# Sorted experts in two halves of the tokens, and the expert's register loaded a block ahead

## What is computed

```python
def _L1_ffn_ref(x, W_router, b_router, W1, b1, W2, b2):      # 8 experts, top 2, D_FF = 512
    logits = x @ W_router + b_router
    # top 2 experts of each token, softmax over their two logits -> weights
    ...
    # for each expert: y = relu(x @ W1[e] + b1[e]) @ W2[e] + b2[e]
    # output = sum over the two chosen experts of weight * y
...
x = _layernorm(x + _L1_attn_ref(x, ...), axis=-1)
x = _layernorm(x + _L1_ffn_ref(x, L1_ffn_W_router, L1_ffn_b_router, L1_ffn_W1, L1_ffn_b1, L1_ffn_W2, L1_ffn_b2), axis=-1)
```

## Time and profile before

| | us |
|---|---|
| median of 3 runs | 1996.16 (1993.97 to 1998.4) |
| the profiled execution, its own time | 1996.44 |
| its span in the trace | 1994.7 |
| of that, ahead of the last layer | 1784.6 |
| the last layer | 210.1 |

### The profile page before, as it was taken

The page is one execution under the profiler, slowest core; times in us unless marked ns, Lnnn a source line. Parts: engine busy times, 40 slices in busy tenths (PEclk is TensorE's granted clock), DMA queues, the critical chain, the costliest instruction groups (busy, mean ns, idle before and its releaser), DMA issues. The chain is left out here.

```text
span 1994.7 us, 42267 instructions
## 1 busy us (share of the span) xinstructions
PE 1715.1 (86%) x15741; PEld 1456.9 (73%) x15741; DVE 1396.7 (70%) x3204; ACT 991.3 (50%) x2605; POOL 600.6 (30%) x978
## 2 busy tenths in 40 slices
PE   3599999899999999999994597999999999997593
PEld 2487778778787787887773465788888888886583
DVE  4688777787777877778774676566666666654466
ACT  2255555455555555555552223565666666541242
POOL 6255335553355543455532000000000000013441
PEclk9799999999999999999997698999999999997697
DMA  5122232223331334313230101990000000011122
GB/s 191 52 70 62 73 83 65 52 62 72 83 73 44 69 75 73 83 43 73 64 73 22 75 1 30 148 5 1 1 1 2 1 1 2 1 61 57 50 59 82
DMA packets 148047, 106.71 MB, mean 53 GB/s; under 512 B 32972, under 2 KB 136216, under 8 KB 146952
## 3 DMA queue, kind: packets, MB, share of 16 engines
q1 hardware_dynamic: 145576, 99.37, 24.0%
q0 software_dynamic: 2272, 4.67, 0.7%
HBM read 86.91 MB, written 17.10 MB: 52 GB/s over the span
## 5 line engine op out<-in xcount | busy, mean ns | idle before, releaser
L577 POOL TENSOR_TENSOR kfull<-kt,pair_rows 128x512 f32<-128x512 f32 x128 | 144.0, 1125 | 515.2 <-ACT kt L365 505.3
L345 PE MATMUL ps<-xT,taps 128*128 128x128 f32 x2176 | 294.1, 278 | 0.1
L345 PEld LDWEIGHTS ps<-xT,taps 128*128 128x128 f32 x2176 | 274.7, 196 | 7.8 <-issue 7.4
L830 ACT COPY wt<-ps 32x128 f32<-32x128 f32 x512 | 131.7, 257 | 260.0 <-PE ps L726 253.5
L1560 DVE TENSOR_REDUCE b_nmax<-ps 128x1 f32<-128x128 f32 (+7 forms) x256 | 180.5, 752 | 73.0 <-PE ps L1397 73.0
L873 DVE TENSOR_TENSOR prod<-ps,mt 128x128 f32<-128x128 f32 x512 | 147.3, 288 | 75.2 <-PE ps L737 60.1
L726 PE MATMUL ps<-ident,w 128*128 128x128 f32 x512 | 162.3, 317 | 34.2 <-ACT wt L830 17.7
L1537 POOL COPY b_spread<-b_inv 128x256 f32<-128x256 f32 x64 | 25.8, 403 | 512.9 <-DVE b_inv L1563 512.9
L876 DVE TENSOR_REDUCE w<-prod 128x32 f32<-128x128 f32 x512 | 146.6, 286 | 17.5
L726 PEld LDWEIGHTS ps<-ident,w 128*128 128x128 f32 x512 | 87.9, 172 | 84.9 <-DVE w L876 73.7
L1489 ACT ACTIVATE b_prob_long<-ps,b_nmax 128x1024 f32<-128x1024 f32 (+3 forms) x128 | 121.4, 953 | 55.7 <-DVE b_nmax L1560 55.7
(11 more groups left out here) (280 smaller groups left out, 3839.0 us busy)
## 6 DMA issues: line engine op xcount, KB each, us to landing
decay<-ends_dram SPq DMA_DIRECT2D x256, 128.0 KB, 5.6
gn<-near_dram SPq DMA_DIRECT2D x34, 384.0 KB, 7.0
rr<-rates_dram SPq DMA_DIRECT2D x34, 256.0 KB, 4.5
sq<-rstd_dram SPq DMA_DIRECT2D x17, 512.0 KB, 3.7
slots_dram<-zero SPq DMA_DIRECT2D x1, 8704.0 KB, 62.5
wtap<-in_taps SPq DMA_DIRECT2D x4, 1024.0 KB, 11.7
f_w<-in_f_w SPq DMA_DIRECT2D x2, 2048.0 KB, 11.5
s_xb<-slots_dram SPq DMA_DIRECT2D x39, 64.5 KB
```

What stands on the lines that cost most here:

```text
L345: mm = pe.matmul(part, lhsT=taps[:, tap, t * P:(t + 1) * P], rhs=xT[:, :, columns(at_next) - LOOK + tap:columns(at_next) - LOOK + tap + TS ...
L577: nc.gpsimd.tensor_tensor(kfull[:, n % 4, :, :], kt[:, n % 2, :].unsqueeze(1).to_broadcast([P, G, P]), cst["pair_rows"][:, :].unsqueeze(2) ...
L830: nc.scalar.copy(wt[rows, b, :], ps[rows, 2, 0:P]).then_inc(wt_kept[b], 1)
```

## The change

`HALVES` is 2. Parts 0 and 1 are the first half, with its own regions in `x_dram`, its own table and 23 blocks, parts 2 and 3 are the second half with 23 more: 46 blocks. The first half's blocks start when its rows have been sent; `choose(3)`, `place_rows(3)`, part 3's sends and the second table are done in the loop, between blocks. The table's code is split in two functions. The reading of the expert's register is taken out of `stage` and put one block earlier. The orders of the head on TensorE, ScalarE and VectorE are loops now, with the parts strictly in turn. The mixing of the first half's tokens happens in the loop, at every second block of the second half, and its norm behind the loop. All stores come behind the last `load_rows`. The table of rows in HBM grows from 17408 to 18432 rows, which are blanked during the second attention.

```diff
-HALVES = 1
+HALVES = 2
...
-                for s in range(PARTS - PG):
-                    store(s)
                 load_rows(HALVES - 1)
-                for s in range(PARTS - PG, PARTS):
+                for s in range(PARTS):
                     store(s)
...
-                project(0)
-                project(1, range(0, 2))
-                turn_x(0)
-                logit(0)
-                project(1, range(2, GT))
-                positions(0)
-                project(2)
-                turn_x(1)
-                logit(1)
-                project(3, range(0, 2))
-                positions(1)
-                project(3, range(2, GT))
-                turn_x(2)
-                logit(2)
-                positions(2)
+                for s in range(PARTS):
+                    project(s, range(0, 2) if s else range(GT))
+                    if s:
+                        turn_x(s - 1)
+                        logit(s - 1)
+                        project(s, range(2, GT))
+                        positions(s - 1)
                 turn_x(3)
                 logit(3)
                 if HALVES == 1:
...
-                squares(0)
-                root(0)
-                keep_x(0)
-                squares(1)
-                root(1)
-                squares(2)
-                keep_x(1)
-                root(2)
-                squares(3)
-                keep_x(2)
-                root(3)
-                keep_x(3)
+                for s in range(PARTS):
+                    squares(s)
+                    root(s)
+                    keep_x(s)
...
-                    if k == 2:
+                    if k == 5:
                         act.wait_ge(S["gaps"], PARTS)
                         nc.scalar.activation(share[:, 1, :], best[:, :, 1], ACT.Exp).then_inc(S["exp_done"], 1)
...
-                out_squares(PARTS - PG)
-                for s in range(PARTS - PG + 1, PARTS):
+                for s in range(PARTS):
                     out_squares(s)
-                    out_root(s - 1)
-                out_root(PARTS - 1)
+                    out_root(s)
...
-                def stage(k):
+                def expert_of(k):
                     if k % BLOCKS == 0:
                         dve.wait_ge(S["table_done"], k // BLOCKS + 1)
+                    return dve.value_load(table_i[0:1, 1, k:k + 1], min_val=0, max_val=NE - 1)
+
+                def stage(k, e):
...
-                    e = dve.value_load(table_i[0:1, 1, k:k + 1], min_val=0, max_val=NE - 1)
...
+                def finish(first, last):
+                    for s in range(first, last + 1):
+                        if s < last:
+                            centre(s, "out_centred")
+                        if s > first:
+                            variance(s - 1, "out_squared", "out_summed")
+                            scale(s - 1, "out_rooted", "out_done")
...
-                choose(0)
-                place_rows(0)
-                add_projected(1)
-                centre(1, "centred")
-                variance(1, "squared", "summed")
-                scale(1, "rooted", "in_done")
-                for s in range(2, PARTS):
+                for s in range(1, PARTS):
+                    choose(s - 1)
                     add_projected(s)
                     centre(s, "centred")
-                    choose(s - 1)
+                    place_rows(s - 1)
                     variance(s, "squared", "summed")
-                    place_rows(s - 1)
                     scale(s, "rooted", "in_done")
                     if HALVES > 1 and s == PG:
+                        count_blocks(0)
                         make_table(0)
...
+                stage(0, expert_of(0))
+                e = expert_of(1)
                 for k in range(K):
                     g, kk = divmod(k, BLOCKS)
                     if k + 1 < K:
-                        stage(k + 1)
+                        stage(k + 1, e)
+                    if k + 2 < K:
+                        e = expert_of(k + 2)
                     if HALVES > 1 and k == 2:
                         place_rows(3)
                     rectify(k)
+                    if HALVES > 1 and k == 0:
+                        choose(3)
                     if k >= 1:
                         keep_y(k - 1)
-                    if HALVES > 1 and k == 5:
+                    if HALVES > 1 and k == 4:
+                        count_blocks(1)
+                    if HALVES > 1 and k == 8:
                         make_table(1)
-                    if k == 8:
+                    if k == 12:
                         share_out()
...
+                    if g and 5 <= kk < 21 and kk % 2:
+                        n = (kk - 5) // 2
+                        if n % GT == 0:
+                            dve.wait_ge(yl_in[n // GT], 16)
+                        mix(n)
                 keep_y(K - 1)
...
+                finish(0, PARTS - PG)
+                for s in range(PARTS - PG, PARTS):
+                    mix_part(s)
+                    centre(s, "out_centred")
+                    if s > PARTS - PG:
                         variance(s - 1, "out_squared", "out_summed")
+                        scale(s - 1, "out_rooted", "out_done")
+                variance(PARTS - 1, "out_squared", "out_summed")
+                scale(PARTS - 1, "out_rooted", "out_done")
```

More of the change, by code:

```diff
@@ L1774, in positions @@
                     for t in range(1, GT):
-                        pe.matmul(small(s)[:, 32 + t * NE:64], lhsT=ones[:, :], rhs=mine[:, 0:(GT - t) * NE], start=False,
-                                  stop=(t == GT - 1), skip_group_check=True)
+                        mm = pe.matmul(small(s)[:, 32 + t * NE:64], lhsT=ones[:, :], rhs=mine[:, 0:(GT - t) * NE], start=False,
+                                       stop=(t == GT - 1), skip_group_check=True)
                     for t in range(GT):
@@ L1975, in place_rows, with count_blocks @@
                     ts(slot_i[:, s, :, :], pair[:, :, :], float(g * STRETCH), None, ALU.add).then_inc(S["slotted"], 1)
-                def make_table(g):
-                    mine = slice(g * BLOCKS, (g + 1) * BLOCKS)
+                def count_blocks(g):
                     ch.step(tt(held[:, :], seen[:, g, PG, :], region[:, :], ALU.subtract))
@@ L1990, in make_table @@
                     ch.step(ts(jump[:, :], blocks[:, :], -float(P), float(SLOTS), ALU.mult, ALU.add))
+                def make_table(g):
+                    mine = slice(g * BLOCKS, (g + 1) * BLOCKS)
                     by = [P, BLOCKS, NE]
@@ L2070, in _ @@
                     place_rows(3)
+                    count_blocks(0)
                     make_table(0)
-                    stage(0)
-                else:
-                    stage(0)
-                    choose(3)
+                stage(0, expert_of(0))
+                e = expert_of(1)
                 for k in range(K):
@@ L2082, in _ @@
                     rectify(k)
+                    if HALVES > 1 and k == 0:
+                        choose(3)
                     if k >= 1:
                         keep_y(k - 1)
-                    if HALVES > 1 and k == 5:
+                    if HALVES > 1 and k == 4:
+                        count_blocks(1)
+                    if HALVES > 1 and k == 8:
                         make_table(1)
-                    if k == 8:
+                    if k == 12:
                         share_out()
-                    if g:
-                        if 6 <= kk < 14:
-                            if kk in (6, 10):
-                                dve.wait_ge(yl_in[(kk - 6) // GT], 16)
-                            mix(kk - 6)
-                        if kk == 10:
-                            centre(0, "out_centred")
-                        if kk == 13:
-                            variance(0, "out_squared", "out_summed")
-                        if kk == 14:
-                            centre(1, "out_centred")
-                        if kk == 16:
-                            scale(0, "out_rooted", "out_done")
-                        if kk == 17:
-                            variance(1, "out_squared", "out_summed")
-                        if kk == 20:
-                            scale(1, "out_rooted", "out_done")
@@ L2106, in _ @@
-                keep_y(K - 1)
-                lead = PARTS - PG
-                for s in range(lead, PARTS + 2):
-                    if s < PARTS:
-                        mix_part(s)
-                        centre(s, "out_centred")
-                    if lead <= s - 1 < PARTS:
+                    if g and 5 <= kk < 21 and kk % 2:
[3 more added lines that the diff above has]
+                        mix(n)
```

11 lines of the change are left out of this document (removed).

## The result

The change makes the kernel 1.5% faster: 1965.7 us median (1965.2 to 1967.96, 4 runs), beside 1997.28 for the kernel before on the same chip, a ratio of 0.9847 with a 95% interval of 0.983 to 0.9864. 1967 was predicted, in a range of 1956 to 1985. The profiled execution took 1965.2, its span is 1963.5, 31.2 less than before. U is the start of the first up.

A forecast was written before the change was run, and what follows sets the result against it. VectorE was taken to set the loop's 2.31 us block, with the register load exposed, between a waiting head and tail. Head -32.8, loop +12.2 and tail -8.7 summed to -29.3 from 1996.44: 1967 us, range 1956 to 1985.

The forecast's parts named there:

- first four blocks: Loop start: choose(3), positions(3) and place_rows(3) delay the first blocks; 13.0 us from first up to up(4), against 8.9 before.
- a plain turn, 41 times: Loop: with the register load ahead, TensorE sets the turn at 1.90 us; 41 blocks make 77.9 us.
- mix(0), with its wait: Loop, k = 28: first mix waits for the first half's rows, 1.3 us (bounds 0 and 3); each mix adds 0.4.
- mixes 1 to 7: Loop, every second block: each 0.75 us mix exceeds VectorE's slack by 0.3 to 0.4, counted as 0.4 us each.
- hitches: Loop: allowance of 1.5 us for slower copies while POOL's queue is full and small hitches (bounds 0 and 3.5).
- tail: After the loop: two norms fill the wait for last results, then two parts remain; 21.6 us against 30.3, -8.7.
- The register load: VectorE, each block: load behind the previous block's copies removes about 0.6 of the 0.81 us hole, leaving 0.2.
- the load stays exposed: Rival, loop: the load waits for the engine, VectorE's 2.31 us a block stays; 1987 us, chance 0.12.
- The head: Before the loop: the first half starts early, first up at 1839.7 against 1872.54 us, -32.8 (bounds -36 and -24).
- The cold head: Rival, head: PE stays at 1.2 GHz from part 1's logits until some us into the loop; 1978 us, chance 0.14.
- POOL: POOL's queue in the loop: part 3's sends, paired with results, end near U+28; no stall, 3 us to spare.
- The rule of the Trainium skill: Rival, loop: VectorE copy and POOL send share ports, the second blocks fully; 35 us more, 2002 us, chance 0.03.

The follow-up runs named there:

- experiments 1 and 2: 1: changed kernel with the register load back in `stage`, 1984.26 us; 2: kernel before with only the load moved one block ahead, 1980.97 us.
- the control: The changed kernel, nothing altered, run again on a third chip beside the kernel before (1998.26 us): 1979.18 us, ratio 0.9908.
- the run that was to tell: The changed kernel with 21 of the head's 24 sends of rows to slots left out, on a fourth chip: 1963.93 us, ratio 0.9828.

## Why the prediction was right, step by step

| term | predicted | measured |
|---|---|---|
| first up (U) | 1839.7 | 1838.53 |
| first four blocks | 13.0 | 11.8 |
| a plain turn, 41 times | 1.90 | 1.90 |
| two table pieces | 3.2 | 3.3 |
| share_out | 0.35 | 0.40 |
| mix(0), with its wait | 1.7 | 4.05 |
| mixes 1 to 7 | 2.8 | 3.4 |
| hitches | 1.5 | -0.1 |
| last up to last keep_y's end | 3.6 | 3.5 |
| loop | 104.0 | 104.3 |
| tail | 21.6 | 20.7 |

A term of the loop is worked out as the interval between ups less 1.90 for each block, for example 3.49 + 1.97 - 3.80 = 1.66 for the first table piece.

*The register load.* Right in place, size and cause; experiments 1 and 2 show it from both sides. The rival "the load stays exposed" falls; its price of 1987 was near what undoing the load's place gives, 1984.

*The head.* Followed step by step it held within 1.2 us all along: choose(1) from 1813.12 to 1816.12 (1813.4 to 1816.4 predicted), place_rows(1) done at 1820.27 (1820.5), the table at 1826.17 (1826.7), the norm of part 3 at 1834.15 (1835.1). PE was at 0.50 in the last 4.3 us, as I had assumed. The cold head did not come in this form. On two chips something like it came, first up 1846 to 1849, but started by late signals and not by the order of the work; that the price I had given, 1978, is near the 1979 of the control is luck.

*The first four blocks.* Mis-sized by 1.2: the choice was ready at U+5.3 (U+5.4 predicted), and PE came back to full clock during the second up (1.29, the next 1.06), so that the positions ended at U+7.2, the early one of the two times I had given (7.4 and 9). place_rows(3) was done at U+8.7 for 9.4 to 10.1, and up(4) came at U+11.8 for 12.4 to 14.

*The mix.* The one term clearly wrong, 2.35 short. The wait itself was 2.08 for 1.3, inside its bounds; what the step left out is the clock: behind a stand of 2.21 us PE was granted 0.53 from 1905.74 to 1909.10, and each of the next two products took 0.8 us more. It was offset by the allowance for hitches, of which nothing was needed: while part 3's sends were in the queue some copies still took up to 0.68 for 0.49, but within VectorE's slack. The sum of the loop, 104.3 for 104.0, is right by that luck: terms of +2.35 and +0.6 (the mixes) against -1.6 (hitches) and -1.2 (first blocks). The head and the tail came 1.2 and 0.9 shorter than predicted.

*POOL.* Part 3's sends ended at 1867.3, U+28.8 (U+28 predicted), and no row load was waited for. The overlap of copy and send costs 0.21 us a block, paid by the send, which has 0.72 us to spare. The rule of the Trainium skill (SBUF — State Buffer, "Who interferes with whom") that the later of the two is blocked fully is not what the rows show for send and copies as a whole: the send that starts 0.08 us behind a copy, with 0.35 us of that copy and 0.75 us of both copies left, took only 0.21 more, and the second copy took 0.49 beside it as it did alone (at 1844.10, with no send under way). When within its 0.96 us a send needs the ports, no row shows.

*The tail.* Two norms took 6.9 us (7.4), the two parts 11.6 (11.8), the end 2.4.

## What to carry to other kernels

Look at what stands between the last instruction of a turn and the first of the next on the engine that sets the turn: a register load placed there left a hole of 0.81 us in VectorE's turn and made the turn 2.32; one block earlier the hole was 0.20 and the turn 1.90. More, smaller pieces for an earlier start pay only if the work ahead of the first piece is put in order for it: halves under the old head gave 0 to 1.3 us, with the new head 13 to 15, whether a block took 2.32 or 1.90. A short wait that TensorE is made to sit out must be priced with the clock it loses.

## What the hardware showed that was not expected

- A wait of 2.21 us on PE was followed by products at 1.86 and 1.92 us for 1.06; waits of 1.43 and 0.83 by products at 1.13. In the control a wait of 2.85 was followed by products at 1.13, 1.73 and 1.91.
- Of a copy and a send that overlap in a plain block, the one that starts second is the longer: copy 0.65 for 0.43 when the send is 0.54 us ahead, send 1.17 for 0.96 when the copy is 0.08 ahead. Neither waits for the other's end. It is no rule for all rows: in the earlier trace rows the send is 0.13 us ahead of the copy, and it is the send that takes 1.09.
- The same program took 1965.7 us on one chip and 1979.2 on another, while the kernel before took 1997.3 and 1998.3. In the slower one's trace signals of TensorE reach VectorE and ScalarE 0.7 to 4.5 us late, from the head's sends of rows to slots to 3.3 us behind the start of the last one; later there are none. The cause is open: the kernel before was not traced there, and the run that was to tell fell on a chip that does not show it.
